# Twelve-block transformer on one core: TensorE multiplies the unit matrix while it waits

## The reference

```python
def _layernorm(x, axis=-1, eps=1e-05):
    m = jnp.mean(x, axis=axis, keepdims=True)
    v = jnp.var(x, axis=axis, keepdims=True)
    return (x - m) / jnp.sqrt(v + eps)
...
    x = x + _L0_xattn_ref(_layernorm(x, axis=-1), ctx_1024, ...)
    x = x + _L0_attn_ref(_layernorm(x, axis=-1), ...)
    x = x + _L0_ffn_ref(_layernorm(x, axis=-1), ...)
    ...
    x = x + _L3_ffn_ref(_layernorm(x, axis=-1), ...)
```

```python
        losses = jnp.mean((recon - x[None]) ** 2, axis=(2, 3))
        top1 = jnp.argmin(losses, axis=0)
...
        locations = jnp.cumsum(mask, axis=0) - 1
        mask = mask * (locations < C)
        loc_oh = jax.nn.one_hot(locations, C, dtype=probs.dtype)
```

## Time and profile before

| | |
|---|---|
| median of 3 runs | 1254.36 us (1253.89 to 1255.26) |
| the profiled execution | 1256.31 us, of it span 1254.3 us |
| mean granted TensorE clock | 0.898 of full speed |
| TensorE busy | 1081.7 us, 86% of the span, 4822 MATMUL |
| VectorE, ScalarE, GpSimd busy | 575.9, 426.8, 312.7 us |
| moved by DMA | 39.99 MB, mean 32 GB/s |

### The profile page before, as it was taken

How to read it: one execution, slowest core, us unless ns; L and a number is a source line. 1 busy time by engine, 2 the same in 40 slices (tenths; PEclk the granted TensorE clock), 3 DMA queues, 4 the chain that set the end, 5 groups by cost and what they waited for, 6 DMA issues and landing times.

```text
span 1254.3 us, 13184 instructions
## 1 busy us (share of the span) xinstructions
PE 1081.7 (86%) x4822; PEld 605.2 (48%) x4822; DVE 575.9 (46%) x1003; ACT 426.8 (34%) x705; POOL 312.7 (25%) x93
## 2 busy tenths in 40 slices
PE   7997788976799866964969999999999999998468
PEld 4664334644656533633846444444444444444334
DVE  3886763225467642224344334443443444343344
ACT  3664403315387541411225322322322232322111
POOL 0000000000000000000002666646655665564000
PEclk9998799988799875985989999999999999999659
DMA  8200000030000010050000000000000000000100
GB/s 346 90 1 1 0 1 1 1 135 1 2 1 2 20 82 0 1 240 11 1 1 1 21 17 21 17 17 17 21 17 15 19 21 13 17 21 1 73 0 9
DMA packets 21366, 39.99 MB, mean 32 GB/s; under 512 B 2496, under 2 KB 18880, under 8 KB 19648
## 3 DMA queue, kind: packets, MB, share of 16 engines
q1 hardware_dynamic: 21312, 39.25, 8.4%
HBM read 38.98 MB, written 0.26 MB: 31 GB/s over the span
## 4 chain that ended last, share of the span: by engine, by line
PE 54%; DVE 5%; ACT 4%; issue 1%; POOL 1%; POOLq 0%; DVEq 0%
PE PSUM L1970 18%; PE PSUM L1974 17%; PE PSUM L1518 2%; PE PSUM L2095 2%; PE PSUM L2017 1%; PE PSUM L1553 1%; PE PSUM L1884 1%; PE PSUM L1940 1%; PE PSUM L1464 1%; PE PSUM L2109 1%; ACT ARENA L623 1%; POOL RSTD L379 1%; PE PSUM L2030 1%; PE PSUM L2101 1%; PE PSUM L1958 1%
## 5 line engine op out<-in xcount | busy, mean ns | idle before, releaser
L435 POOL TENSOR_TENSOR ARENA<-ARENA 128x2048 f32<-128x2048 f32 x64 | 289.0, 4516 | 176.7 <-ACT ARENA L708 176.6
L1312 DVE TENSOR_TENSOR ARENA<-PSUM,RK 128x512 f32<-128x512 f32 x256 | 176.3, 692 | 281.3 <-PE PSUM L1970 278.9
L1970 PE MATMUL PSUM<-ARENA,CK 128*128 128x512 f32 x512 | 252.8, 597 | 0.7 <-ACT ARENA L704 0.7
L1974 PE MATMUL PSUM<-ARENA,CK 128*128 128x512 f32 x512 | 251.2, 593 | 2.1 <-ACT ARENA L708 2.1
L708 ACT ACTIVATE ARENA<-ARENA,CK 128x2048 f32<-128x2048 f32 x64 | 128.1, 2002 | 313.1 <-DVE ARENA L1312 313.1
L1974 PEld LDWEIGHTS PSUM<-ARENA,CK 128*128 128x128 f32 x512 | 96.7, 190 | 126.5 <-issue 107.9
L1970 PEld LDWEIGHTS PSUM<-ARENA,CK 128*128 128x128 f32 x512 | 96.6, 191 | 118.8 <-issue 97.5
L379 POOL TENSOR_TENSOR RSTD<-VE,MHALF 128x4 f32<-128x4 f32 x15 | 15.1, 1009 | 509.7 <-DVE VE L790 509.7
L1482 PE MATMUL PSUM<-WK,CT 128*128 128x512 f32 x256 | 126.1, 616 | 0.0
L811 DVE TENSOR_REDUCE RK<-SQ 128x8 f32<-128x512 f32 x128 | 84.8, 683 | 34.4 <-ACT SQ L465 34.3
L465 ACT ACTIVATE SQ<-PSUM 128x512 f32<-128x512 f32 x128 | 75.4, 594 | 46.5 <-PE PSUM L1482 46.5
(11 more groups left out here) (389 smaller groups left out, 1300.5 us busy)
## 6 DMA issues: line engine op xcount, KB each, us to landing
CT<-in_ctxT SPq DMA_DIRECT2D x4, 1024.0 KB, 9.9
CK<-in_l0f_experts SPq DMA_DIRECT2D x1, 4096.0 KB, 22.1
CK<-in_ctxk SPq DMA_DIRECT2D x1, 4096.0 KB, 12.1
ARENA<-in_l2f_experts SPq DMA_DIRECT2D x2, 2048.0 KB, 8.2
CK<-in_ctxT SPq DMA_DIRECT2D x64, 64.0 KB, 1.8
CK<-in_ctxr SPq DMA_DIRECT2D x64, 64.0 KB, 1.8
ARENA<-in_l2f_experts SPq DMA_DIRECT2D x1, 3072.0 KB, 14.7
WB<-in_wb SPq DMA_DIRECT2D x1, 2834.5 KB, 11.0
```

What stands on the lines that cost most here:

```text
L435: nc.gpsimd.tensor_tensor(LS[b % 2], LS[b % 2], PR[:, k % 2, :], ALU.add)\
L1312: ve.tensor_tensor(PR[:, k % 2, c * 512:(c + 1) * 512].rearrange("p (j n) -> p j n", j=4), PSUM[:, c % 2, :].rearrange("p (j n) -> p j n", ...
L1970: mm(bank(c % 2), CTT[:, k, :], qpb[:, b, c * 512:(c + 1) * 512], start=True, stop=True)\
L1974: return mm(bank(4 + c), CKT[:, k, :], PR[:, k % 2, c * 512:(c + 1) * 512], start=first, stop=final, skip_group_check=True)
```

## The change

Three helpers are new in TensorE's list. `stay_busy(n, k)` issues n products of the 128x128 unit matrix with itself into the first 128 columns of bank k, which nobody reads before the bank's next real use; no signal goes out. `busy_until_variance(norm, n, after)` issues n of them, waits for the variance of the normalisation numbered `norm`, and issues `after` more. `busy_until_sum(block, n)` issues n and waits until that block has been added to x. They are called ahead of waits that are there already; the new waits are for signals that come before those.

```diff
+            def stay_busy(n, k=0):
+
+                for _ in range(n):
+                    mm(PSUM[:, k, 0:P], ident, ident, start=True, stop=True)
+
+            def busy_until_variance(norm, n, after):
+
+                stay_busy(n)
+                nc.tensor.wait_ge(sem("variance"), norm)
+                stay_busy(after)
+
+            def busy_until_sum(block, n):
+
+                stay_busy(n)
+                nc.tensor.wait_ge(sem("x_ready"), block)
+
...
@@ core_pe
+                    if groups == 1:
+                        stay_busy(11)
                     nc.tensor.wait_ge(sem("probs"), PE.due("probs"))
@@ long_pe
                     if masked:
+                        if b == 0:
+                            stay_busy(8, 4)
                         nc.tensor.wait_ge(sem("long_scores_taken"), PE.due("long_scores_taken"))
                     else:
+                        if b == 0:
+                            stay_busy(10, 4)
+                            nc.tensor.wait_ge(sem("long_shift"), B + 1)
+                            stay_busy(7, 4)
                         nc.tensor.wait_ge(sem("long_probs"), PE.due("long_probs"))
                     if b + 1 < B:
                         scores(b + 1)
                     if masked:
+                        if b % 2 == 0:
+                            stay_busy(8 if b == 0 else 5, 4)
                         nc.tensor.wait_ge(sem("long_probs"), PE.due("long_probs"))
...
+            busy_until_variance(2, 6, 5)
             turn_pe()
...
+            stay_busy(8, 3)
             nc.tensor.wait_ge(sem("l0a_u"), PE.due("l0a_u"))
...
+            stay_busy(4, 3)
             nc.tensor.wait_ge(sem("l0a_y"), PE.due("l0a_y"))
...
+            busy_until_sum(3, 7)
+            busy_until_variance(4, 6, 5)
             turn_pe()
...
+            stay_busy(2)
             turn_pe(ACC)
...
+            stay_busy(8)
             nc.tensor.wait_ge(sem("l1f_losses"), PE.due("l1f_losses", n=NA))
             mm(PSUM[:, 5, 0:32], w("ones"), SM[:, 0:32], start=True, stop=True).then_inc(sem("l1f_loss"), PE.sends("l1f_loss"))
+            stay_busy(20)
             nc.tensor.wait_ge(sem("l1f_masked"), PE.due("l1f_masked"))
...
+            stay_busy(11)
             nc.tensor.wait_ge(sem("l2a_h"), PE.due("l2a_h"))
...
+            busy_until_variance(9, 6, 12)
+            busy_until_sum(8, 0)
+            busy_until_variance(10, 5, 5)
             turn_pe()
...
             last.then_inc(sem("l2f_places"), PE.sends("l2f_places"))
+            stay_busy(18)
             nc.tensor.wait_ge(sem("l2f_onehot"), PE.due("l2f_onehot"))
...
             finish_values()
+            stay_busy(8)
             finish_turn()
+            stay_busy(2)
             finish_out()
```

More of the change, by code:

```diff
@@ L1749, in _ @@
             tail_pe(w("l1x_Wo"))
+            busy_until_variance(5, 6, 5)
             turn_pe()
@@ L1783, in _ @@
                     lambda g, j: PSUM[:, 6, (4 * g + j) * HD:(4 * g + j + 1) * HD], norms_from=64)
+            stay_busy(5)
             turn_pe(ACC)
@@ L1786, in _ @@
             tail_pe(w("l1a_Wproj"))
+            busy_until_variance(6, 6, 5)
             turn_pe()
@@ L1821, in _ @@
             last.then_inc(sem("block_out"), PE.sends("block_out"))
+            busy_until_variance(7, 6, 5)
             turn_pe()
@@ L1836, in _ @@
             tail_pe(w("l2x_WvT"))
+            busy_until_sum(7, 5)
+            busy_until_variance(8, 5, 5)
             turn_pe()
@@ L1935, in _ @@
             nc.tensor.wait_ge(sem("dma_wc"), PE.due("dma_wc"))
+            busy_until_variance(11, 7, 5)
             turn_pe()
@@ L2063, in _ @@
             finish_values()
+            stay_busy(8)
             finish_turn()
+            stay_busy(2)
             finish_out()
+            busy_until_variance(12, 6, 12)
+            busy_until_sum(10, 0)
+            busy_until_variance(13, 5, 5)
             turn_pe()
@@ L2078, in _ @@
                     lambda g, j: V3[:, j, :], lambda g, j: PSUM[:, 6, j * P:(j + 1) * P])
+            busy_until_variance(14, 9, 5)
             turn_pe()
@@ L2081, in _ @@
             tail_pe(w("l3a_Wfc"))
+            busy_until_variance(15, 6, 5)
             turn_pe()
```

## The result

Four executions of the changed kernel took 1205.31 us in the median (1199.44 to 1213.89), four of the kernel before beside them 1254.34. The ratio is 0.961, with a 95% interval of 0.954 to 0.969; the forecast was 1208 us in a range of 1197 to 1229. The execution that was profiled is the longest, 1213.89 us, its span 1211.8.

What follows compares the result with a forecast made beforehand. TensorE's half-speed clock in stages of short products with waits was taken as the bound. A full gain of 56.6 us, -1.0 -2.4 +1.0 -1.5 -6.2, left 46.5: from a median of 1254.4 to 1208 us, range 1197 to 1229.

Steps and rivals of the forecast that it cites:

- term 4: End of layer 1's cross attention: output projection stays slow behind 32-column work despite added products, -1.0 us of gain.
- term 8: Normalisations: the clock still lapses at one in five of 13, at 2.4 us each, -6.2 us of gain.
- What bounds it: Outside layer 3's long attention, short products with stops leave TensorE at half speed: 258.5 us at 0.50, 165.8 busy.
- The price of a product: Each added 128-column product costs 0.23 us at the high clock, 0.43 at the low, free if done before its wait ends.
- Terms 1 to 3: All places with added products: half of 134.2 us busy at low clock, less latency and unawaited work, gives 56.6 us.
- Term 5: Routing of layer 2: 16-column products slow for half, the 18 products behind them overrun by 0.9; -2.4 us in all.
- Term 6: End of layer 3's cross attention: 64-column products stay slow, eight products overrun by 0.8, output projection gains 1.8; together +1.0 us.
- Term 7: Last routing: narrow logits with nothing added behind them cost 1.5 us of the experts' first products.
- term 3: Work nobody waits for, including 4.2 us of spreads in layer 0's gate: 4.6 us less gain.
- rival A: Clock falls at nearly every normalisation, making the lapses cost 31 us and not 6: 1233 us, chance 0.16.
- Rival C: Identity products, nearly all zeros, do not hold the clock; added groups overrun their waits everywhere: slower, 1278 us, chance 0.03.
- Rival B: No lapses at normalisations and narrow work costs less, so the losses there and at the last routing vanish: 1200 us, chance 0.20.

Runs made afterwards that it cites:

- the repeated run: The changed kernel unaltered, run again for six executions and a second trace: 1206.26 us, ratio 0.9595 to the kernel before.
- the normalisations alone: Changed kernel with only the 170 added products at the normalisations, the other 143 removed: 1224.77 us, ratio 0.9751 to the kernel before.
- 16 columns: Changed kernel with all 313 added products at the same places but 16 columns wide, not 128: 1267.07 us, ratio 1.0097 to the kernel before.
- nine products: Changed kernel with nine added products, not six, before the variance of each normalisation: 1211.73 us, ratio 0.9634 to the kernel before.

## Why the prediction was right

The profiled execution gained 42.4 us against its own kind (1256.3 to 1213.9), where the sum said 46.5; the medians gained 49.0, where it said 46. The mechanism came as forecast, but that the totals lie so close is in part luck: 8.0 us in the profiled execution were in no term, and terms 4 and 8 were too dark. Step by step:

- **What bounds it**: right. The loop of layer 3 did not move, the time came from the stages with waits, and the time at 0.50 fell from 258.5 to 69.7 us (56.4 in the repeated run), forecast some 60 to 90.
- **The price of a product**: right. 626 passes take 83.1 us, 0.133 each with those at the low clock, against 0.116 in the earlier trace rows; at the normalisation shown, 12 take 1.50 and 10 take 1.38, where 1.4 and 1.15 were said. The doubt drawn from the Trainium skill, "TensorE: Matmul & The Clock Gate", its section on LDWEIGHTS, under which the adapters' 20 products would overrun a wait of 5.5, isn't borne out: 40 passes took 4.71 us there and TensorE then stood idle for 0.92.
- **Terms 1 to 3, the full gain of 56.6**: about right. In the profiled execution the real work on TensorE shrank by 52.6 us. The adapters' products take 6.90 us (448.27 to 455.17) and took 12.68, 5.8 less, where 5.1 was said of the part in the earlier trace rows. The first scores went to 3.44 from the third on; on the first the clock fell, so 1.2 came there and not 3.1.
- **Term 4, end of layer 1's cross attention, -1.0**: not so in the profiled execution, where the output projection is fast; in the repeated run the clock falls there at 304.7, and the stage is 1.2 us longer. Of the eight profiles of kernels with all the products at 128 columns, five have that fall.
- **Term 5, routing of layer 2, -2.4**: right in place. Its overrun of 0.9 came as 0.9 in the profiled execution and as 2.0 in the repeated run, so that match is luck. The 16-column products take 3.90 us and not 4.46, forecast 3.4.
- **Term 6, end of layer 3's cross attention**: too dark. In the profiled execution it went as said, with eight products in 3.31 us (3.4) and an overrun of 0.3, not 0.8. But of nine profiles of kernels with these eight products, seven have them at 2.00 us, at the high clock, and the way from the loop's end to VectorE's closing copy (L1358) 2.2 us shorter (34.8 against 37.0 us): the 64-column work ahead of them mostly did not lose the clock. Nor did it in the profiles with the normalisations alone and with 16 columns, though it had in the kernel before. So some 2 us gained here may lie in where the clock happened to fall, and not in the filled wait.
- **Term 7, last routing, -1.5**: the size fits, the place doesn't. From VectorE's first instruction of the routing (L1410) to the end are 40.6 us in the profiled execution and 38.9 in five of the eight profiles. But in the profiled one the experts' first products run at the high clock, and the 1.7 us go where it falls later, at 1178.5, behind 16-row products. Behind the logits it falls in the repeated run (1164.8) and with nine products.
- **Term 8, lapses at normalisations, -6.2**: too dark, and not by chance one in five. One normalisation of 13 has a fall behind it in the profiled execution, the seventh (465.1), and the stage is 72.5 us, where it is 70.9 in the only one of the eight profiles without that fall (two products behind each turn): 1.7 us. The fall in the recurrence (533.4) is at no normalisation; by the same comparison it costs 1.8 (26.0 against 24.2). Seven of the eight profiles have both falls, so they belong to these places. That the clock holds through the turns speaks against the second rule weighed, that transposes don't count as activity (the Trainium skill, the same page, Part 4: PE-mode transpose): rival A, which hung on it, would have put the clock down at all 13.
- **What the sum lacked**: the experts of layer 2, -8.0 us in the profiled execution. I had treated narrow work as work that cannot lift the clock (terms 4 to 7) and only after a wait. That the clock can fall on such work while TensorE is busy, and then stay down for 17 us, is what the profile shows in its place; the stretch from 583.3 to 587.7 in the earlier trace rows shows only that such work leaves a low clock low. Against it the gate of layer 0 gained 2.4 us, though term 3 took its spreads for work that nobody waits for; that wasn't taken apart. How often the experts fall isn't known: of the twelve profiles of kernels with products only this one has it, but an execution of 1213.56 us in the repeated run, with the same mean clock of 0.972, was not profiled. So 8.0 us is its price in one execution. The median lies 2.7 us under the forecast, which fits terms 6 and 8 and a fall that most executions don't have.

Rival C falls with the price and the sign; the 16-column run shows that it was a real danger of a neighbouring design, not of this one. Rival B's 1200 is what the best executions of the changed kernel take (1199.4, 1199.7), so it isn't a rival mechanism but the lower end of the same spread.

Open: what decides in which execution the clock falls where. Kernels that differ by nothing ahead of a place show it there or not, and no profiled row tells them apart beforehand. Not tried: products of other widths, and operands that aren't mostly zeros.

## What to carry to other kernels

Where the granted clock is low in stages of short products with waits between them, count TensorE's busy time in those stretches: half of it is the most that full-width products on an unread bank can give back (here 83 us, of which 49 came, 4%, with 313 products), and they cost nothing while they end before the wait does. Make them as wide as the real work and fill nearly the whole wait: half as many kept a third of the gain, an eighth of the width made it slower than nothing. Put none where the next engine already waits for TensorE, and look after narrow work (16, 40 or 64 columns) separately, because it can lose the clock while busy.

## What the runs showed of the hardware

- A mix of 40-column passes, 40-row passes and transposes ran for 17 us at 1.00 before, where it began with the clock up, and for 17.1 us at 0.50 in one execution of the changed kernel, where the clock had fallen on the 40-column passes just ahead. Busy 100% in both.
- 16-column products with a full weight load each leave TensorE busy and the clock down: 255 us at 0.50 with 227 busy.
- With the clock mostly up, executions of one program spread more: ten of the changed kernel took 1199.4 to 1213.9 us. The kernel before, timed beside the runs, took 1253.9 to 1257.0 in the 15 executions beside these ten, and up to 1262.4 in later ones. A single execution can't rank two such kernels; six left intervals of 0.3% to either side.
- The start of the program, before anything that the change touches, took from 22.8 to 27.7 us in the profiles (up to the first token sums). That is up to 5 us between two executions that no added product explains.
